# One row product moved from VectorE to GpSimd and ScalarE, the mixes put behind the masks, the last norm on VectorE, one norm's statistics in two parts

## The chip, the cores and the metric

One NeuronCore of one Trainium2 chip runs the whole program. The metric is the device time of one execution in microseconds (us); lower is better. Engines are named PE (TensorE matmul), PEld (TensorE weight load), DVE (VectorE), ACT (ScalarE), POOL (GpSimd) and SP (SyncE, which here only issues DMAs).

## What is computed

One block of a transformer over x of shape 8 x 1024 x 128, all float32. `mod` comes from a small product of `c`. The inner functions, cut to what matters:

```python
h = layernorm(x) * (1 + ca) + sa            # ca, sa: 128 channels, one set per batch
q, k, v, g = h @ Wq.T, h @ Wk.T, h @ Wv.T, h @ Wg.T     # 8 heads, 64 / 64 / 128 / 128 wide
q, k = rotary(q), rotary(k)
o = (q k^T / 8 * decay, causal) v           # retention, no softmax, per head
o = (o - mean) * rsqrt(var + eps) * gn_weight + gn_bias
x = x + ga * ((o * silu(g)) @ Wo.T)
h = layernorm(x) * (1 + cb) + sb
xr, xk = mix of h[t] and h[t-1] by mu_r, mu_k
x = x + gb * (sigmoid(xr @ W_r.T) * (relu(xk @ W_k.T)**2 @ W_v.T))
```

## The kernel before

The 8192 tokens are 64 chunks of 128 (`NCHUNK`), four chunks make a group of 512 tokens (`NGROUP` = 16), two groups a batch. The five engines run five programs that are written out by hand: a prologue, then a loop over `steps` in which every engine does a fixed list of pieces, and a tail for the last group. `due(step - 11, GC, LAST)` says in which step of its engine a piece for a group or chunk comes. Engines meet only through semaphores, so the order of an engine's list is the order in which it works, and a wait stops all that stands behind it on that engine.

In a step PE transposes keys (`transpose_k`), does the causal part of a chunk's retention (`attend`), the scores of the next (`scores`), the part from the running state (`recall`), the new state, the projections q, v, gate, k, and the output projection of older heads. `attend(i)` writes the two PSUM banks `O_E` and `O_O`, and for that it waits until the heads of chunk i-1 were read out of them: `norm_heads(i-1)` on DVE, semaphores `n_E` and `n_O`. The way there starts at the end of `recall(i-1)`: ACT squares (L803), DVE sums (L1145), POOL adds and takes the power -1/2 (`head_rstd`, L1442 and L1445), DVE multiplies (`norm_heads`, L1152).

The first layer norm has two forms. Groups 0 to 3 normalize x by rows and turn it on PE. Groups 4 to 15 (`BY_ROWS`) turn only the statistics: they go through DRAM and come back spread over all partitions (`row_of[:, 0, :]` is the reciprocal deviation, `row_of[:, 1, :]` the shift), while x itself is loaded already turned (`x_turned`, channels on partitions). For these twelve groups

- ACT `scale_rows` (L764) multiplies and shifts `row_of[:, 1, :]` by the channels' factors,
- DVE `apply_rows` (L1071) does `h_full = x_turned * (1 + ca) * row_of[:, 0, :]`,
- POOL `add_rows` (L1410) adds `row_of[:, 1, :]`,
- ACT `round_h` and POOL `low_h` (L1404) split it in a high and a low part for the projections.

In the second half of the block `mix_shift_r` and `mix_shift_k` (DVE, L1164 and L1170) make the two mixes, `round_mix` (ACT, L847) rounds the second, and `split_mix` (DVE, L1179) takes the rest. `mask` (DVE, L1125) puts the causal mask on the scores; `norm_stats` (DVE, L1051 and L1054) takes mean and variance of a group.

The tail does the last group in two parts of two chunks: residual, statistics (DVE), `last_rstd` (POOL), `last_apply` (ACT, L864), `last_transpose` (PE, L548), `last_modulate` (ACT, L884), `last_mix` (DVE, L1229 and L1232), two products, `last_square`, a third product, `last_product` (DVE, L1245 and L1249), store. `keep_busy` are matmuls whose result nobody reads, put before the two `last_transpose`.

## Time and profile before

| | |
|---|---|
| time, median of 3 runs | 751.33 us (750.21 to 752.49) |
| the profiled execution's own time | 750.83 us |
| its span, first to last instruction | 749.0 us |
| PE, PEld busy | 98%, 86% |
| DVE, ACT, POOL busy | 81%, 64%, 81% |
| granted TensorE clock | full in every slice |

The span is what the views of the trace show; the 1.8 us between it and the time lie around it. Busy shares are means over stages that differ, so the views by stretch and by wait are read beside them.

### The profile page before, as it was taken

The numbers are of one execution on the slowest core, as the hardware profiler recorded it, in microseconds if no ns is written. First come the engines' busy times: TensorE is split into PE (matmuls) and PEld (weight loads), VectorE is DVE, ScalarE is ACT, GpSimd is POOL, SyncE is SP. The second block draws the span as 40 slices with busy tenths as digits, with TensorE's granted clock in tenths as the row PEclk, the third lists the DMA queues.
The fourth block names the chain that finished last, engine by engine and source line by source line (L and its number), as shares of the span: only waits on it lengthen the run. The fifth ranks groups of instructions, "written<-read, shape, count | busy, mean of one in ns | idle before, by whom it ended". The sixth has DMA issues, their size and how long they took to land.

```text
span 749.0 us, 29004 instructions
## 1 busy us (share of the span) xinstructions
PE 735.4 (98%) x12123; PEld 643.0 (86%) x12123; DVE 605.7 (81%) x1265; ACT 482.4 (64%) x932; POOL 604.3 (81%) x655
## 2 busy tenths in 40 slices
PE   8989999999999999999999999999999999999997
PEld 7778888888889889888888988988888888988886
DVE  4997688878888887988888898887898878787546
ACT  4566666575665666666666665766666666656665
POOL 5877779789698897988889797888979889787641
PEclk9999999999999999999999999999999999999999
DMA  7611020200202121030211303021020201001001
GB/s 249 193 31 20 13 59 10 65 18 16 79 17 79 25 73 30 10 93 13 75 25 26 81 13 87 9 79 31 13 84 17 73 16 30 18 9 31 24 15 29
DMA packets 59809, 35.15 MB, mean 47 GB/s; under 512 B 36664, under 2 KB 54432, under 8 KB 59680
## 3 DMA queue, kind: packets, MB, share of 16 engines
q1 hardware_dynamic: 58960, 32.51, 16.8%
q8 instruction: 96, 1.57, 0.9%
q10 hardware_dynamic: 720, 0.80, 0.3%
q14 instruction: 33, 0.27, 0.1%
HBM read 20.66 MB, written 4.25 MB: 33 GB/s over the span
## 4 chain that ended last, share of the span: by engine, by line
PE 81%; DVE 10%; issue 3%; ACT 2%; POOL 2%; DMA 1%; SPq 0%; DVEq 0%
PE ring L332 45%; PE outs L332 13%; PE O_E L332 12%; PE ring L347 7%; PE O_O L332 2%; DVE gn_sum L1145 2%; DVE N L1152 1%; DVE delta L1170 1%; ACT N L803 1%; DVE S L1139 1%; DMA N<-in_w_vT 1%; PE ring L397 1%; DVE mix_r L1164 1%; DVE rot_k L1115 1%; DVE sin_k L1118 1%
## 5 line engine op out<-in xcount | busy, mean ns | idle before, releaser
L1452 POOL TENSOR_TENSOR y<-y,gate 128x512 f32<-128x512 f32 x120 | 152.4, 1287 | 29.4 <-ACT y L815 29.4
L1435 POOL TENSOR_TENSOR rot_k<-rot_k,sin_k 128x256 f32<-128x256 f32 x128 | 106.2, 850 | 26.5 <-DVE sin_k L1118 25.8
L332 PEld LDWEIGHTS outs<-wo_gated,y 128*128 128x128 f32 x992 | 119.8, 192 | 6.7 <-DVE y L1191 0.5
L779 ACT ACTIVATE v<-ring 64x512 f32<-64x512 f32 x128 | 76.0, 594 | 75.3 <-PE ring L332 74.3
L332 PE MATMUL outs<-wo_gated,y 128*128 128x128 f32 x992 | 121.7, 275 | 0.1
L1145 DVE TENSOR_REDUCE gn_sum<-N 128x4 f32<-128x512 f32 x118 | 75.5, 681 | 43.4 <-ACT N L803 43.4
L1445 POOL TENSOR_TENSOR gn_rstd<-gn_var,minus_half 128x8 f32<-128x8 f32 x64 | 105.3, 1645 | 5.0
L787 ACT ACTIVATE kT<-ring 128x512 f32<-128x512 f32 x64 | 38.3, 598 | 103.0 <-PE ring L347 103.0
L815 ACT ACTIVATE y<-ring,gn 128x512 f32<-128x512 f32 x126 | 90.9, 777 | 5.2 <-PE ring L347 5.2
L1125 DVE TENSOR_TENSOR A<-ring,consts 128x256 f32<-128x256 f32 x128 | 48.2, 417 | 56.2 <-PE ring L332 56.2
L1429 POOL TENSOR_TENSOR qT<-qT,swapped 128x512 f32<-128x512 f32 x60 | 77.2, 1287 | 14.8 <-DVE swapped L1101 14.6
L808 ACT ACTIVATE gate<-ring 128x512 f32<-128x512 f32 x128 | 76.8, 601 | 3.6 <-PE ring L332 1.2
L1139 DVE TENSOR_TENSOR S<-ring,S 128x512 f32<-128x512 f32 x112 | 76.8, 685 | 2.9 <-PE ring L332 1.0
L332 PE MATMUL O_E<-v,A 64*64 64x128 f32 x992 | 68.0, 275 | 0.6 <-DVE N L1152 0.6
L332 PE MATMUL O_O<-v,A 64*64 64x128 f32 x992 | 68.0, 275 | 0.0
L332 PE MATMUL ring<-v,rot_k 64*64 64x128 f32 x960 | 67.5, 270 | 0.3 <-DVE A L1125 0.3
L332 PE MATMUL ring<-v,k_odd 64*64 64x128 f32 x960 | 67.1, 269 | 0.0
L332 PE MATMUL O_E<-S,qT 64*64 64x128 f32 x928 | 65.3, 269 | 0.1
L332 PE MATMUL O_O<-S,qT 64*64 64x128 f32 x928 | 64.6, 269 | 0.0
L332 PEld LDWEIGHTS ring<-v,rot_k 64*64 64x64 f32 x960 | 57.6, 133 | 0.8 <-issue 0.8
L332 PEld LDWEIGHTS ring<-v,k_odd 64*64 64x64 f32 x960 | 57.9, 133 | 0.0
L332 PEld LDWEIGHTS O_E<-v,A 64*64 64x64 f32 x992 | 53.1, 132 | 4.8 <-DVE N L1152 0.7
(199 smaller groups left out, 2107.9 us busy)
## 6 DMA issues: line engine op xcount, KB each, us to landing
k_odd<-rot_k SPq DMA_DIRECT2D x128, 64.0 KB, 2.2
row_of<-written_rows SPq DMA_DIRECT2D x12, 512.0 KB, 4.0
X<-in_x SPq DMA_DIRECT2D x16, 256.0 KB, 4.3
out<-X SPq DMA_DIRECT2D x15, 256.0 KB, 2.4
x_turned<-in_xT SPq DMA_DIRECT2D x12, 256.0 KB, 4.4
key_tables<-in_const SPq DMA_DIRECT2D x7, 256.0 KB, 5.1
rotary_q<-in_const_q SPq DMA_DIRECT2D x2, 512.0 KB, 6.4
gates<-stored_rows SPq DMA_DIRECT2D x8, 128.0 KB, 3.1
```

Of the source, the lines that this page charges most:

```text
L332: return e.matmul(o, lhsT, rhs, start=start, stop=stop, skip_group_check=True)
L347: done = e.transpose(bank[:, at_column:at_column + HALF], tokens[rows, :], ident[rows, rows])
L779: done = e.activation(v[halves(half), i % 2, 1, :, :], by(PAIRS, bank_of["v", odd, i][halves(1 - half), :]), ACT.Copy)
L808: e.activation(gate[:, n % 2, :], bank_of["gate", n][:, :], ACT.Silu).then_inc(sem["gate"])
L815: e.activation(in_halves(by(GC, y[:, n % NY, :])), from_halves(bank_of["n", n // 2], n % 2, GC), ACT.Identity, bias=gn[:, 1, h:h + 1], sca ...
L1125: e.tensor_tensor(A[:, odd, :, :], by(PAIRS, bank_of["kT", i][:, odd, W // 2:W]), causal.unsqueeze(1).broadcast_to([P, PAIRS, HALF]), ALU. ...
L1139: e.tensor_tensor(new, added, old, ALU.add).then_inc(sem["S"])
L1145: e.tensor_reduce(gn_sum[:, i % 2, odd, :], N[:, i % NN, odd, :, :], AXIS.X, ALU.add).then_inc(sem["sum_" + eo])
L1429: e.tensor_tensor(q, q, swapped[:, :], ALU.add).then_inc(sem["qT"])
L1435: done = e.tensor_tensor(turned[:, n, :, :], turned[:, n, :, :], sin[:, n, :, :], op)
L1445: e.tensor_tensor(gn_rstd[:, i % 2, :, :].rearrange("p e a -> p (e a)"), gn_var[:, i % 2, :, :].rearrange("p e a -> p (e a)"), minus_half[ ...
L1452: e.tensor_tensor(y[:, n % NY, :], y[:, n % NY, :], gate[:, n % 2, :], ALU.mult).then_inc(sem["y"])
```

## The change

Five things are edited.

1. `apply_rows` moves from DVE to POOL and loses the factor by channels; that factor becomes an activation on ACT in `scale_rows`, in place on `x_turned`. `add_rows` stays on POOL, but stands between the two `gate_head` of its step and no longer in front of `rotate_k`.
2. In the loop DVE does `mix_shift_k` behind the two masks, and ACT does `round_mix` behind the squares of the next step.
3. In the tail `last_apply` is a two-scalar operation on DVE (subtract the mean, multiply by the reciprocal deviation); the negated mean and the shift go away; the mix r, the relu and the tanh are written in another order; the last `ffn_out` goes from POOL to DVE; 2 + 3 idle matmuls stand where 5 + 4 stood.
4. `norm_stats` is split in `norm_stats` and `norm_mv`. In the prologue the statistics of group 2 are taken right behind `add_state(0)`, and only `norm_mv(2, 0)` stays where both were.
5. In the prologue the masks of chunk 2 stand in front of `norm_heads(0, 1)`.

The diff, cut (the semaphores that come and go are left out):

```diff
         def scaled_rows(g):
-            return 2 * (g - BY_ROWS) + 2
+            return 3 * (g - BY_ROWS) + 3
...
-            keep_busy(O[1][:, :, :].rearrange("p n v -> p (n v)"), 5, True)
+            keep_busy(O[1][:, :, :].rearrange("p n v -> p (n v)"), 2, True)
             last_transpose(0)
-            keep_busy(O[1][:, :, :].rearrange("p n v -> p (n v)"), 4, True)
+            keep_busy(O[1][:, :, :].rearrange("p n v -> p (n v)"), 3, True)
             last_transpose(1)
             last_k(0)
+            last_k(1)
             last_r(0)
-            last_k(1)
...  scalar, scale_rows
                 at.wait_ge("rows_read", 32 * (g - BY_ROWS + 1))
+                e.activation(x_turned[:, :], x_turned[:, :], ACT.Copy, scale=mod_cols[:, 1, b:b + 1]).then_inc(sem["rows_act"])
                 e.activation(row_of[:, 1, :], row_of[:, 1, :], ACT.Identity, bias=mod_cols[:, 0, b:b + 1],
...  scalar, loop
                 for i in due(step, 1, NCHUNK, 4):
                     square(i, 1)
+                for g in due(step - 10, GC, LAST):
+                    round_mix(g)
...
-                for g in due(step - 9, GC, LAST):
-                    round_mix(g)
...  vector
-            def apply_rows(g):
-                e.scalar_tensor_tensor(out=h_full[:, :], in0=x_turned[:, :], scalar=mod_cols[:, 1, b:b + 1], in1=row_of[:, 0, :],
-                                       op0=ALU.mult, op1=ALU.mult).then_inc(sem["rows_applied"])
...
+            def last_apply(part):
+                at.wait_ge("last_rstd", part + 1)
+                at.wait_ge("n0T", NGROUP)
+                at.wait_ge("n1T", LAST)
+                for j in range(GC)[chunks_of(part)]:
+                    e.tensor_scalar(normed[:, j, :], X[:, LAST % NX, j, :], ln_mv[:, 1, j, 0:1], ln_rstd[:, 1, j:j + 1],
+                                    ALU.subtract, ALU.mult).then_inc(sem["last_apply"])
...
+            def last_ffn_out():
+                xg = X[:, (LAST - 1) % NX, :, :]
+                e.tensor_tensor(xg, xg, product, ALU.add).then_inc(sem["ffn_out"])
...  vector, prologue
             add_state(0)
+            norm_stats(2, 0)
             rotate_k(2)
...
             norm_heads(0, 0)
-            norm_heads(0, 1)
             mask(2, 1)
             mask(2, 0)
+            norm_heads(0, 1)
             rotate_q(5)
             add_state(2)
-            norm_stats(2, 0)
+            norm_mv(2, 0)
...  vector, loop
-                for g in due(step - 11, GC, LAST):
-                    mix_shift_k(g)
...
                 for i in due(step, 1, NCHUNK, 5):
                     mask(i, 0)
+                for g in due(step - 11, GC, LAST):
+                    mix_shift_k(g)
...
-                for g in due(step + 6, GC, NGROUP, BY_ROWS):
-                    apply_rows(g)
...  gpsimd
+            def apply_rows(g):
+                at.wait_ge("rows_read", 32 * (g - BY_ROWS + 1))
+                at.wait_ge("rows_act", scaled_rows(g))
+                e.tensor_tensor(h_full[:, :], x_turned[:, :], row_of[:, 0, :], ALU.mult).then_inc(sem["rows_applied"])
...
                 for g in due(step + 8, GC, NGROUP, BY_ROWS):
-                    add_rows(g)
+                    apply_rows(g)
                 for i in due(step + 4, 1, NCHUNK, 7):
                     rotate_k(i)
...
                     gate_head(2 * i)
+                for g in due(step + 8, GC, NGROUP, BY_ROWS):
+                    add_rows(g)
...
             last_rstd(1)
-            ffn_out(LAST - 1)
```

POOL's list in the step of a group by rows (`y` is `gate_head`, `rot_k` is `rotate_k`, `gn_rstd` is the power in `head_rstd`), before:

```order
L1461 TENSOR_TENSOR delta<-h2T 128x512
L1429 TENSOR_TENSOR qT<-qT,swapped 128x512
L1410 TENSOR_TENSOR h_full<-h_full,row_of 128x512
L1435 TENSOR_TENSOR rot_k<-rot_k,sin_k 128x16x16 x2
L1452 TENSOR_TENSOR y<-y,gate 128x512 x2
L1442 TENSOR_TENSOR gn_var<-gn_sum,consts 128x8
L1445 TENSOR_TENSOR gn_rstd<-gn_var,minus_half 128x8
```

and the same place of the changed kernel:

```order
L1477 TENSOR_TENSOR delta<-h2T 128x512
L1445 TENSOR_TENSOR qT<-qT,swapped 128x512
L1422 TENSOR_TENSOR h_full<-x_turned,row_of 128x512
L1451 TENSOR_TENSOR rot_k<-rot_k,sin_k 128x16x16 x2
L1468 TENSOR_TENSOR y<-y,gate 128x512
L1426 TENSOR_TENSOR h_full<-h_full,row_of 128x512
L1468 TENSOR_TENSOR y<-y,gate 128x512
L1458 TENSOR_TENSOR gn_var<-gn_sum,consts 128x8
L1461 TENSOR_TENSOR gn_rstd<-gn_var,minus_half 128x8
```

One instruction of 128x512 more stands between `qT` and `gn_rstd`. On ACT, the step before that one has the scaling of the rows and a second-half norm (`normed`) in front of the copy of the turned keys (`kT`); in the changed kernel:

```order
L783 ACTIVATE v<-ring 128x512
L809 ACTIVATE gate<-ring 128x512
L764 ACTIVATE x_turned<-x_turned,mod_cols 128x512
L765 ACTIVATE row_of<-row_of,mod_cols 128x512
L751 ACTIVATE normed<-X,ln_rows 128x128 x4
L788 ACTIVATE kT<-ring 128x2x4x64
```

The `x_turned` row is new, the others stood there in the same order. The end of DVE's list, changed kernel, from the statistics of the second part (`swapped` is the mix k and later its square, `turned` the mix r and later the tanh):

```order
L1200 BN_STATS ln_stats<-X 128x6 x2
L1203 BN_AGGR ln_mv<-ln_stats 128x2 x2
L1211 TENSOR_SCALAR normed<-X,ln_mv,ln_rows 128x128 x2
L1172 SCALAR_TENSOR_TENSOR delta<-mix_r,ring 128x512
L1211 TENSOR_SCALAR normed<-X,ln_mv,ln_rows 128x128 x2
L1222 TENSOR_TENSOR h_full<-h2T 128x256
L1224 SCALAR_TENSOR_TENSOR swapped<-h_full,mu,h2T 128x256
L1222 TENSOR_TENSOR h_full<-h2T 128x256
L1224 SCALAR_TENSOR_TENSOR swapped<-h_full,mu,h2T 128x256
L1229 SCALAR_TENSOR_TENSOR turned<-h_full,mu,h2T 128x256
L1241 TENSOR_TENSOR swapped<-swapped 128x256
```

The four `normed` are new on DVE. Behind these rows come the second mix r, the second square, the 128x512 addition of the last `ffn_out`, and two pairs of `last_product`.

## Rows read from the trace of the kernel before

**Rows 1.** The page, part 1: busy us, share and instructions of each engine.

```profile
PE 735.4 (98%) x12123; PEld 643.0 (86%) x12123; DVE 605.7 (81%) x1265; ACT 482.4 (64%) x932; POOL 604.3 (81%) x655
```

**Rows 2.** Stretches: length, busy us and instructions of PE, PEld, DVE, ACT, POOL.

```profile
300.00:400.00 100.00, 99.91 (x1696) 87.87 (x1694) 85.82 (x173) 65.48 (x118) 87.55 (x96) 1.00 0.17 41
...
700.00:749.00 49.00, 43.88 (x504) 37.52 (x502) 28.38 (x66) 30.64 (x58) 19.37 (x23) 1.00 0.07 20
```

**Rows 3.** Timeline of POOL, 427 to 448: start, us, instruction, [idle before <-releaser].

```profile
427.32 1.42 POOL L1435 TENSOR_TENSOR rot_k<-rot_k,sin_k 128x256 f32<-128x256 f32 x2 [0.52 <-DVE sin_k L1118]
...
430.05 1.28 POOL L1452 TENSOR_TENSOR y<-y,gate 128x512 f32<-128x512 f32 x1 [1.31 <-ACT y L815]
...
439.59 1.33 POOL L1410 TENSOR_TENSOR h_full<-h_full,row_of 128x512 f32<-128x512 f32 x1
440.88 2.33 POOL L1435 TENSOR_TENSOR rot_k<-rot_k,sin_k 128x256 f32<-128x256 f32 x2
443.18 2.54 POOL L1452 TENSOR_TENSOR y<-y,gate 128x512 f32<-128x512 f32 x2
...
445.97 1.65 POOL L1445 TENSOR_TENSOR gn_rstd<-gn_var,minus_half 128x8 f32<-128x8 f32 x1
```

**Rows 4.** Timeline of DVE in the same step.

```profile
439.71 1.76 DVE L1164 SCALAR_TENSOR_TENSOR mix_r<-delta,mu,h2T 128x512 f32<-128x512 f32 x1
...
448.25 0.68 DVE L1152 TENSOR_TENSOR N<-O_O,gn_rstd 128x512 f32<-128x512 f32 x1
```

**Rows 5.** Timelines: PE's next attend, then POOL and PE one group later.

```profile
449.91 0.32 PE L332 MATMUL O_E<-v,A 64*64 64x128 f32 x1
...
490.40 1.65 POOL L1445 TENSOR_TENSOR gn_rstd<-gn_var,minus_half 128x8 f32<-128x8 f32 x1
...
494.59 0.32 PE L332 MATMUL O_E<-v,A 64*64 64x128 f32 x1
```

**Rows 6.** Timelines, last chunk: POOL's power and the attend that waits for it.

```profile
708.58 1.64 POOL L1445 TENSOR_TENSOR gn_rstd<-gn_var,minus_half 128x8 f32<-128x8 f32 x1
...
711.68 0.29 PE L332 MATMUL O_E<-v,A 64*64 64x128 f32 x1 [0.60 <-DVE N L1152]
```

**Rows 7.** Timelines of ACT and PEld, the step before a step by rows.

```profile
426.54 1.64 ACT L751 ACTIVATE normed<-X,ln_rows 128x128 f32<-128x128 f32 x4
428.64 0.60 ACT L787 ACTIVATE kT<-ring 128x512 f32<-128x512 f32 x1 [0.46 <-PE ring L347]
...
429.34 0.38 PEld L332 LDWEIGHTS ring<-qT,kT 64*64 64x64 f32 x16
```

**Rows 8.** Groups by form, 200 to 700: busy us, mean ns, idle before.

```profile
L764 ACT ACTIVATE row_of<-row_of,mod_cols 128x512 f32<-128x512 f32 x10 | 8.2, 823 | 0.0
...
L770 ACT ACTIVATE hT_hi<-h_full 128x512 fp32r<-128x512 f32 x10 | 6.2, 622 | 0.0
...
L1164 DVE SCALAR_TENSOR_TENSOR mix_r<-delta,mu,h2T 128x512 f32<-128x512 f32 x11 | 15.3, 1394 | 0.0
...
L1071 DVE SCALAR_TENSOR_TENSOR h_full<-x_turned,mod_cols,row_of 128x512 f32<-128x512 f32 x10 | 7.4, 739 | 0.0
```

**Rows 9.** Timelines of DVE and PE in the prologue.

```profile
27.30 0.69 DVE L1115 TENSOR_TENSOR rot_k<-ring,key_tables 128x512 f32<-128x512 f32 x1 [0.74 <-PE ring L332]
...
41.60 0.86 DVE L1051 BATCH_NORM_STATS2 ln_stats<-X 128x6 f32<-128x128 f32 x4
42.38 0.36 DVE L1054 BATCH_NORM_AGGREGATE ln_mv<-ln_stats 128x2 f32<-128x6 f32 x4
...
43.97 0.47 PE L347 MATMUL ring<-consts,rot_k 64*128 64x64 f32 x8 [1.16 <-DVE qT L1098]
```

**Rows 10.** Timelines of ACT and DVE in the tail.

```profile
738.42 0.88 ACT L864 ACTIVATE normed<-X,ln_rows 128x128 f32<-128x128 f32 x2
...
740.54 0.62 DVE L1229 TENSOR_TENSOR h_full<-h2T 128x256 f32<-128x256 f32 x1 [1.28 <-ACT h2T L884]
...
746.26 0.42 DVE L1249 TENSOR_TENSOR X<-X,h_full 128x256 f32<-128x256 f32 x1
```

More of the change, by code:

```diff
@@ L857, in load_tables @@
                 e.dma_start(key_tables[:, c, :, :, :].rearrange("p k h d -> p (k h d)"), columns).then_inc(sem[tables(c)[0]], 16)
-            def last_apply(part):
-                at.wait_ge("last_shift", part + 1)
-                at.wait_ge("n0T", BY_ROWS)
-                at.wait_ge("n1T", LAST)
-                for j in range(GC)[chunks_of(part)]:
-                    e.activation(normed[:, j, :], X[:, LAST % NX, j, :], ACT.Identity, bias=ln_shift[:, 1, j:j + 1],
-                                 scale=ln_rstd[:, 1, j:j + 1]).then_inc(sem["last_apply"])
             def last_scale(part):
@@ L997, in _ @@
                 last_relu(part)
+            for part in range(PARTS):
                 last_act_r(part)
@@ L1217, in last_stats @@
                 done.then_inc(sem["last_mv"])
-                at.wait_ge("last_mv", part + 1)
-                e.tensor_scalar(ln_neg[:, 1, these], ln_mv[:, 1, these, 0], -1.0, None, ALU.mult).then_inc(sem["last_neg"])
+            def last_apply(part):
[5 more added lines that the diff above has]
+                                    ALU.subtract, ALU.mult).then_inc(sem["last_apply"])
             def last_mix(part):
@@ L1230, in last_mix, with last_mix_r @@
                 at.wait_ge("last_delta", part + 1)
-                for n, what in ((1, "k"), (0, "r")):
-                    e.scalar_tensor_tensor(out=last_mixed[what][:, cols], in0=last_delta[:, cols], scalar=mu[:, n:n + 1], in1=before,
-                                           op0=ALU.mult, op1=ALU.add).then_inc(sem["last_mix_" + what])
+                e.scalar_tensor_tensor(out=last_mixed["k"][:, cols], in0=last_delta[:, cols], scalar=mu[:, 1:2], in1=before,
+                                       op0=ALU.mult, op1=ALU.add).then_inc(sem["last_mix_k"])
+            def last_mix_r(part):
+                cols = tokens_of(part)
+                e.scalar_tensor_tensor(out=last_mixed["r"][:, cols], in0=last_delta[:, cols], scalar=mu[:, 0:1],
+                                       in1=h2T[:, 1, cols], op0=ALU.mult, op1=ALU.add).then_inc(sem["last_mix_r"])
+            def last_ffn_out():
+                xg = X[:, (LAST - 1) % NX, :, :]
+                at.wait_ge("product", LAST)
+                at.wait_ge("ffn_out", LAST - 1)
+                e.tensor_tensor(xg, xg, product, ALU.add).then_inc(sem["ffn_out"])
             def last_square(part):
@@ L1354, in _ @@
             last_stats(1)
+            last_apply(0)
             ffn_product(LAST - 1)
+            last_apply(1)
             last_mix(0)
             last_mix(1)
+            last_mix_r(0)
             last_square(0)
+            last_mix_r(1)
             last_square(1)
+            last_ffn_out()
             last_product(0)
@@ L1476, in last_rstd @@
                                 ).then_inc(sem["last_rstd"])
-                at.wait_ge("last_rstd", part + 1)
-                at.wait_ge("last_neg", part + 1)
-                e.tensor_tensor(ln_shift[:, 1, these], ln_neg[:, 1, these], ln_rstd[:, 1, these], ALU.mult
-                                ).then_inc(sem["last_shift"])
             e.memset(minus_half[:, :], -0.5)
```

21 lines of the change are left out of this document (11 added, 10 removed).

## The prediction

> **What bounds the kernel now.** I read the page's busy shares first. PE has 98%, DVE and POOL 81% each, ACT 64% [rows 1]. The table of stretches then says where PE is not full: from 300 to 400 us it is busy 99.91 of 100 us, in the last 49 us 43.88 [rows 2]. So in the loop nothing done faster on another engine can shorten the time; only a delay that reaches PE can change it, upward. Gains can lie in the prologue and in the tail.
>
> The question for the loop is how much room each step leaves PE. I went through the timelines of POOL, DVE and PE step by step. PE starts `attend` of a chunk when DVE has normed the heads of the chunk before, and DVE needs POOL's `gn_rstd` for that. In the step in which POOL adds the rows, POOL has no idle time from 430.05, where it waited for ACT's y, to the end of `gn_rstd` at 445.97 + 1.65 = 447.62 [rows 3]. PE begins the next attend at 449.91 [rows 5], 2.29 us after it. One group later `gn_rstd` ends at 492.05 and PE begins at 494.59, 2.54 us later [rows 5]. Eleven steps have this form (attends from 182 to 628 us): six with 2.29 to 2.32, five with 2.53 to 2.55. The first of the twelve groups by rows, at 138 us, has 3.7.
>
> How little is enough is seen at the last chunk, where PE really waits: `gn_rstd` ends at 708.58 + 1.64 = 710.22, PE starts at 711.68 [rows 6], so 1.46 us are used by two multiplications of DVE and the signals. The room is therefore 2.29 - 1.46 = 0.83 us in six steps and 2.54 - 1.46 = 1.08 in five.
>
> **The rows on POOL.** In front of `gn_rstd` one more product of 128x512 comes on POOL. The same kind with the same operands' size takes 2.50 us for two, start to end of the y pair (443.18 to 445.68), so 1.25 each [rows 3]. Nothing hides it, since POOL has no idle time there. The sum 1.25 - 0.83 gives 0.42 us of new wait of PE in six steps, 1.25 - 1.08 gives 0.17 in five: 2.5 + 0.85 = **3.4 us**. Behind the waiting `attend` stands all of PE's list, and PE is the bound, so it isn't given back. The add between the two `gate_head` changes the place of a delay, not its length; its second y ends near 447, and PE reads it with the output projection behind the first one at about 448, so that is still in time.
>
> What DVE saves there is its own product, 739 ns [rows 8]. It stood before the norm of the odd heads in the step before, on an engine that isn't waited for there. I cost that at nothing; its cover is POOL's queue, which is what comes last.
>
> Does it relieve POOL? DVE and POOL slow each other: the mixes (`mix_r` 1394 ns on average) take nearly twice the 739 ns of the same instruction in `apply_rows` [rows 8], and the `rot_k` beside them takes 2.33 us where one beside no mix takes 1.42 [rows 3], as DVE's `mix_r` from 439.71 lasts 1.76 [rows 4]. So it is the mixes that POOL pays for, 0.91 us, and the removed product paid nothing extra. The Trainium skill, "SBUF — State Buffer", section "Who interferes with whom", has the rule: a VectorE instruction with two SBUF inputs and a GpSimd instruction that reads SBUF lock each other out for a whole instruction. By that rule the removal of a two-input instruction from VectorE speaks for the change; the row of 739 ns says that here it met no long POOL instruction. The two mixes remain, and POOL is busy wherever they fall, so moving mix k behind the masks moves its 0.4 to 0.5 us and doesn't remove it. That is the first rival below.
>
> **The factor by channels on ACT.** It comes in the step before, in front of `row_of`, four `normed` and the copy of the turned keys. Its duration isn't in the trace: a copy of that size without pointer operands takes 622 ns, one with two (scale and bias) 823 [rows 8]; this one has one, I take the middle, 720, and by the pipelining seen between `normed` (until 428.18) and its neighbours it takes about 0.1 less of ACT's time, 0.62; the bounds are 0.52 and 0.72. The Trainium skill, "ScalarE: Activation LUTs", section "What ACT_TABLE_LOAD costs", says that each [128,1] pointer operand adds about 93 ns; 622 + 93 would be 715, and the rows agree. ACT had 0.46 us idle in front of `kT` [rows 7]. So the copy comes 0.16 late (0.06 to 0.26). It ended at 429.24, and PE loaded the first of these weights at 429.34 [rows 7]; with a signal of 0.05, 0.05 are free. PE waits 0.11 (0.01 to 0.21), twelve times: **1.3 us** (0.1 to 2.5). POOL's chain starts behind ACT's y in this same step [rows 3], so it is late by the part that PE doesn't share, 0.05 in eleven steps: **0.5 us**.
>
> **Mix k and its rounding.** In the loop the masks wait for PE anyway, and the rounding's wait for DVE goes away in front of ACT's squares. Both shorten the way to the sums, but in the steps by rows POOL takes the sums late, and that way is not what PE waits for. Zero in the loop; without the cover it would be a gain of some tenths in five steps, counted in the rival.
>
> **Prologue.** PE idles 1.16 us before 43.97, for a bank that DVE's rotation releases [rows 9]. DVE is busy without pause from 27.3 to there. The statistics of group 2, 41.60 to 42.38, go to 26.6, where DVE idled 0.74 us for PE [rows 9]; x of that group has landed by then. DVE reaches the rotation 0.78 earlier, POOL's reciprocal deviation too. What follows up to 60 us hangs on DVE in the same order. Gain **0.8 us**, the 0.78 of the row (0.2 if the idle time at 26.6 takes less of it; 1.2, the whole of PE's wait, with what the earlier masks of chunk 2 add).
>
> **Tail.** ACT's two `normed` run from 738.42 to 739.30, DVE's first delta starts at 740.54, and the last addition ends at 746.68 [rows 10]. DVE can begin `normed` at 738.3, without the shift on POOL (0.2) and without ACT. I take 0.25 each from the statistics' size, so the first part is ready at 738.8; PE is past its last real products and two idle matmuls at 739.0, transposes until 739.4, ACT gives h2T at 739.95, DVE's delta starts at 740.0. The second part follows at 741.0 where it was 742.3. From there DVE is the bound. Two deltas and two mixes k at 0.46 each, with a wait for the second part (until 741.95), two mixes r and two squares of 0.40 to 0.45 (until 743.7), the `ffn_out` that came from POOL, 0.68 like the 128x512 of [rows 4], then the four of `last_product`, 1.75. That ends at 746.1. Gain **0.55 us** (1.3 if the `ffn_out` falls in a wait; a loss of 0.2 if its 256 KB store, now at 744.4, delays the last ones).
>
> **Sum.** 3.4 + 1.3 + 0.5 - 0.8 - 0.55 = +3.85 on the profiled execution's 750.83 (span 749.0 and 1.8 around it), so 754.7; that execution is 0.5 below the median of 751.33. On the median it is **755.2 us**, 0.5% slower. With the low bounds (PE's wait at the keys 0.1, prologue 1.2, tail 1.3, no lag of POOL's chain) it is +1.0, 752.3; with the high ones (2.5, 0.2, and +0.2) +6.4, 757.7.
>
> **Rivals.** What a measurement can tell from no change is about 0.3%, 2.25 us, so 749.1 to 753.6.
>
> *POOL is relieved.* If the mixes no longer meet POOL's chain, POOL gets back the 0.91 us, the new product costs 0.34, less than the room of 0.83, and PE waits in no step by rows. Left are the keys (0.1 to 1.3), the prologue and the tail: 0 to -1.25. With the tail at its best (0.75 more) and some 0.25 us of small waits gone from PE in the five steps of the second kind, where DVE's sums come earlier, it is -3.3: 748.0. It decides from 0.42 us less in POOL's chain on. For it speaks that the mixes are spread out; against it that POOL has no pause in the stretch, so that a mix must displace something.
>
> *A part only.* The 1.25 us are partly hidden, or ACT's copy costs nothing, and the three gains stand: +1 to +2, 753.
>
> *The delay spreads.* POOL leaves the step 1.25 us late, and the next step's chain, with 4.5 us from `gn_rstd` to attend, has room. But the second y, the low part of h for the next group and the released banks come late as well; if one of them stops PE by another 0.3 us in each of the eleven steps, +7: 758.5.
>
> *The change doesn't do what it says* can't be here; the lists show each move.
>
> **How the numbers follow.** The forecast (waits of PE in the steps by rows, +1.0 to +6.4) 0.55, nearly all of it slower by over 0.3%; a part only 0.17, within; POOL relieved 0.20, of it 0.12 faster by over 0.3% and 0.08 within; the delay spreads 0.08, slower. With 0.01 of the forecast within, faster is 0.12, same 0.26, slower 0.62. The range is 748.8 to 758.0, which leaves out the best part of the relief and most of the spread; the forecast alone has 752.3 to 757.7.
>
> **What the profile after would show.** In a step by rows POOL without a pause, `gn_rstd` ending 1.3 us later against PE's earlier attend, and a wait of PE "O_E <- DVE N" of 0.2 to 0.5, eleven times; the waits before the scores for ACT's `kT` near 0.1, twelve times; the gap before the transposes of chunk 3 near 0.4 to 0.7 instead of 1.16; DVE the chain from 740 on. The prediction is wrong if `gn_rstd` is followed by the attend in more than 1.46 us in these steps, or if `rot_k` beside the mixes falls to 1.42.

## The result, and the profile after

The changed kernel takes 753.38 us (median of 22 executions, 752.17 to 756.4); the kernel before, on the same chips, 751.14 (22 executions, 750.04 to 753.5). The ratio is 1.0034, 95% interval [1.0025, 1.0043]: about 2.5 us slower. The profiled executions differ by 2.2 us of span, 751.2 after against 749.0.

The page's shares of the kernel after, to be held against [rows 1]:

```profile
PE 733.0 (98%) x12119; PEld 644.2 (86%) x12119; DVE 598.8 (80%) x1256; ACT 488.1 (65%) x940; POOL 616.8 (82%) x664
```

DVE has 6.9 us less, POOL 12.5 more, ACT 5.7 more. No engine is full, so this says little; the chain that ended last says more. It follows the work back from the last instruction, with each engine's share of the span, and by line. First the shares before, then both lines after:

```profile
PE 81%; DVE 10%; issue 3%; ACT 2%; POOL 2%; DMA 1%; SPq 0%; DVEq 0%
```

```profile
PE 74%; DVE 10%; POOL 9%; issue 4%; ACT 1%; DMA 1%; ACTq 0%; DVEq 0%
PE ring L332 41%; PE O_E L332 12%; PE outs L332 12%; PE ring L347 6%; POOL y L1468 4%; PE O_O L332 3%; POOL gn_rstd L1461 3%; DVE N L1139 2%; POOL h_full L1426 2%; DVE gn_sum L1132 1%; DVE delta L1157 1%; DVE A L1112 1%; PE ring L397 1%; DMA consts<-in_const 1%; DVE wffn_v L1033 1%
```

POOL's part has grown from 2% to 9%: its products y, `gn_rstd`, and the addition of the rows. PE's waits say where it enters. After, the list of what PE waited for begins with

```profile
PE O_E L332 <- DVE N L1139: 5.6, 11, 0.8
PE ring L347 <- DVE sin_k L1105: 1.1, 1, 1.1
```

Before, the attend waited once in this way, for 0.6 us [rows 6]. Now it is eleven times, 5.6 us together: in ten of the eleven steps by rows, and again at the last chunk. The same stretch as in [rows 2]:

```profile
300.00:400.00 100.00, 99.11 (x1693) 87.79 (x1692) 84.21 (x170) 66.45 (x119) 89.28 (x97) 1.00 0.15 41
```

PE is 0.80 us less busy than before in these 100 us, POOL 1.73 more. Here is POOL's timeline in the step that [rows 3] show, with the two multiplications of DVE and the attend that hang on it:

```profile
440.26 1.33 POOL L1445 TENSOR_TENSOR qT<-qT,swapped 128x512 f32<-128x512 f32 x1
441.54 1.74 POOL L1422 TENSOR_TENSOR h_full<-x_turned,row_of 128x512 f32<-128x512 f32 x1
443.23 1.98 POOL L1451 TENSOR_TENSOR rot_k<-rot_k,sin_k 128x256 f32<-128x256 f32 x2
445.17 1.31 POOL L1468 TENSOR_TENSOR y<-y,gate 128x512 f32<-128x512 f32 x1
446.44 1.29 POOL L1426 TENSOR_TENSOR h_full<-h_full,row_of 128x512 f32<-128x512 f32 x1
447.68 1.30 POOL L1468 TENSOR_TENSOR y<-y,gate 128x512 f32<-128x512 f32 x1
448.94 0.21 POOL L1458 TENSOR_TENSOR gn_var<-gn_sum,consts 128x8 f32<-128x8 f32 x1
449.23 1.65 POOL L1461 TENSOR_TENSOR gn_rstd<-gn_var,minus_half 128x8 f32<-128x8 f32 x1
...
450.91 0.69 DVE L1139 TENSOR_TENSOR N<-O_E,gn_rstd 128x512 f32<-128x512 f32 x1 [3.15 <-POOL gn_rstd L1461]
451.51 0.68 DVE L1139 TENSOR_TENSOR N<-O_O,gn_rstd 128x512 f32<-128x512 f32 x1
...
452.34 0.29 PE L332 MATMUL O_E<-v,A 64*64 64x128 f32 x1 [0.84 <-DVE N L1139]
```

POOL works without a pause. DVE sits idle for 3.15 us until `gn_rstd` ends at 450.88, and PE starts 1.46 us after that, the bare minimum of the last chunk [rows 6], where it had 2.29 before. In ten of the eleven steps this distance is now 1.46 or 1.47.

In the steps of one kind the wait is longer than what the step grows by. The next such step grows by 0.18, and its attend waits 0.50:

```profile
497.19 0.29 PE L332 MATMUL O_E<-v,A 64*64 64x128 f32 x1 [0.50 <-DVE N L1139]
```

With the rows' part alone (`e2_rows_only`, below) that wait is 0.10 or 0.12. The other 0.4 is time that item 2 saved earlier in the same step (shown under the mixes), and PE now spends it waiting here.

Where the 2.2 us of span come from is read off the starts of the 64 attends, each against its counterpart before. The steps by rows from 182 to 628 us are longer by 0.41, 0.18, 0.41, 0.18, 0.43, 0.18, 0.83, 0.18, 0.40, 0.16 and -0.01, together +3.35. (Of the 0.83, which is the step shown, about 0.4 is there once: ahead of these rows POOL idles 0.26 us for nothing that the trace names, and its `qT` and `rot_k` take 0.06 and 0.11 longer than in the other steps of this kind. Why stays open.) The first attend came 0.22 late, and by attend 9 the shift was -0.47, a gain of 0.69; attends 10 and 11 gave +0.11; single steps and the last attend +0.17. The last attend is 3.16 late, and the span ends only 2.2 late, so 0.96 came back in the tail. The 0.22 goes with the clock: in the first 15 us the mean granted clock is 0.89, before it was 1.00. It is no part of the change: in the profiled executions of all fourteen kernels the first attend comes 0 to 0.33 early where those 15 us have 1.00 (five kernels), 0.02 to 0.57 late where they have 0.89 (eight, among them `e2_rows_only` and `e4_factor_on_act`, whose start is the one of before), and 1.38 late at 0.77 (`e5_mixes_only`).

### The profile page after: what moved, and what is told of

Read it like the earlier page. It is cut to its first block, busy times and chain, and to the rows that moved or that the text cites. A ratio compares the mean times of both kernels' runs of the same rounds, so it can differ in the third digit from the quotient of the medians.

```text
span 751.2 us, 29021 instructions
## 1 busy us (share of the span) xinstructions
PE 733.0 (98%) x12119; PEld 644.2 (86%) x12119; DVE 598.8 (80%) x1256; ACT 488.1 (65%) x940; POOL 616.8 (82%) x664
## 3 DMA queue, kind: packets, MB, share of 16 engines
q8 instruction: 96, 1.57, 0.9%
## 4 chain that ended last, share of the span: by engine, by line
PE 74%; DVE 10%; POOL 9%; issue 4%; ACT 1%; DMA 1%; ACTq 0%; DVEq 0%
PE ring L332 41%; PE O_E L332 12%; PE outs L332 12%; PE ring L347 6%; POOL y L1468 4%; PE O_O L332 3%; POOL gn_rstd L1461 3%; DVE N L1139 2%; POOL h_full L1426 2%; DVE gn_sum L1132 1%; DVE delta L1157 1%; DVE A L1112 1%; PE ring L397 1%; DMA consts<-in_const 1%; DVE wffn_v L1033 1%
## 5 line engine op out<-in xcount | busy, mean ns | idle before, releaser
L1468 POOL TENSOR_TENSOR y<-y,gate 128x512 f32<-128x512 f32 x120 | 156.8, 1320 | 30.0 <-ACT y L816 29.9
L1451 POOL TENSOR_TENSOR rot_k<-rot_k,sin_k 128x256 f32<-128x256 f32 x128 | 102.1, 819 | 27.2 <-DVE sin_k L1105 25.8
L1139 DVE TENSOR_TENSOR N<-O_E,gn_rstd 128x512 f32<-128x512 f32 x62 | 42.2, 681 | 31.8 <-POOL gn_rstd L1461 31.7
```

The lines of the kernel that those rows point to most:

```text
L1139: e.tensor_tensor(N[:, i % NN, odd, :, :], heads_of(i)[odd], rstd, ALU.mult).then_inc(sem["n_" + eo])
L1451: done = e.tensor_tensor(turned[:, n, :, :], turned[:, n, :, :], sin[:, n, :, :], op)
L1468: e.tensor_tensor(y[:, n % NY, :], y[:, n % NY, :], gate[:, n % 2, :], ALU.mult).then_inc(sem["y"])
```

## The experiments

Twelve kernels. Each was timed beside the kernel before on the same chip; a shift of an attend is taken from the profiled execution against that of before. "Steps by rows" are the same eleven as above, six of a first kind (10.62 to 10.65 us long before, the last one 10.48) and five of a second (10.81 or 10.82).

### The rows' part alone, and everything but it

`e1_rows_back` is the changed kernel with item 1 undone:

```diff
 ACT scale_rows
-                e.activation(x_turned[:, :], x_turned[:, :], ACT.Copy, scale=mod_cols[:, 1, b:b + 1]).then_inc(sem["rows_act"])
 DVE loop, between norm_heads(i, 0) and norm_heads(i, 1)
+                for g in due(step + 6, GC, NGROUP, BY_ROWS):
+                    apply_rows(g)
 POOL loop
-                    apply_rows(g)
+                    add_rows(g)
 ...
                     gate_head(2 * i)
-                for g in due(step + 8, GC, NGROUP, BY_ROWS):
-                    add_rows(g)
```

> The changed kernel with the rows' product back on VectorE and ScalarE's factor by channels gone; mixes behind the masks, prologue and tail stay changed. Theory (the product in POOL's chain is the whole loss, 3.35 us in the steps by rows; prologue and tail give back 0.65 and 0.96): about -1.5 us against the kernel before, 749.7, and the eleven steps by rows as long as before. Rival (the mixes or the order of the edits cost part of it): between -1 and +1.5 us, and some steps by rows stay longer than before.

Measured: 747.92 us against 750.94, ratio 0.9961 [0.9948, 0.9973], -3.0 us: twice the gain that my theory gave. The steps by rows are not as long as before but shorter, by 2.13 us in all: 0.38 to 0.40 in four of the second kind and 0.26 in the last, the others 0.01 to 0.09. So the rest of the change has a gain in the loop that the changed kernel did not show. The tail's part is as expected (last attend at -1.53, span 2.53 shorter, so 1.0).

`e2_rows_only` is the kernel before with item 1 alone, the reverse of that diff on the other kernel.

> The kernel before with the rows' part alone: factor on ScalarE, product on POOL, addition between the two gate_heads. Theory: +3.35 us, 754.5, PE waiting for the normed heads in the eleven steps by rows by 0.41 and 0.17. Rival (mix k behind the masks is what brings VectorE against POOL's product, or spares it): a loss that is smaller or larger than 3.35 by over 0.7 us.

Measured: 753.95 against 750.94, ratio 1.0041 [1.0029, 1.0054], +3.0 us. The steps by rows take 2.93 us more, 0.37 to 0.40 in four of the first kind, 0.68 in the one near 450 us (again an extra of 0.3), nothing in the last, and 0.13 to 0.15 in the second kind. So item 1 on the kernel before costs 2.9. Put on a kernel that has the other items, it costs 3.35 + 2.13 = 5.5, since it also takes their gain.

`e4_factor_on_act` is the kernel before with only the factor on ACT; DVE keeps a plain product.

```diff
 ACT scale_rows
+                e.activation(x_turned[:, :], x_turned[:, :], ACT.Copy, scale=mod_cols[:, 1, b:b + 1]).then_inc(sem["rows_act"])
 DVE apply_rows
+                at.wait_ge("rows_act", scaled_rows(g))
-                e.scalar_tensor_tensor(out=h_full[:, :], in0=x_turned[:, :], scalar=mod_cols[:, 1, b:b + 1], in1=row_of[:, 0, :],
-                                       op0=ALU.mult, op1=ALU.mult).then_inc(sem["rows_applied"])
+                e.tensor_tensor(h_full[:, :], x_turned[:, :], row_of[:, 0, :], ALU.mult).then_inc(sem["rows_applied"])
```

> The kernel before with the factor by channels on ScalarE alone; the product stays on VectorE as a plain multiplication. Theory from the changed kernel's trace: kT comes at most 0.06 us later, PE loses nothing, 0.0 to +0.3 us. Rival (the term of the prediction): twelve waits of 0.11 us and a late chain on POOL, +1.3 to +1.8 us.

Measured: 750.36 against 750.94, ratio 0.9994 [0.9986, 1.0003]. The term of the prediction, +1.3 us, is outside this interval, and so is +1.8 with the late chain. Nor does the trace show the late chain: `gn_rstd` ends 2.30 to 2.33 us before the attend in the first kind of step and 2.55 or 2.56 in the second, no later than before. ACT in the changed kernel, in the step of [rows 7]:

```profile
427.43 0.74 ACT L764 ACTIVATE x_turned<-x_turned,mod_cols 128x512 f32<-128x512 f32 x1
428.04 0.83 ACT L765 ACTIVATE row_of<-row_of,mod_cols 128x512 f32<-128x512 f32 x1
428.75 1.65 ACT L751 ACTIVATE normed<-X,ln_rows 128x128 f32<-128x128 f32 x4
430.30 0.58 ACT L788 ACTIVATE kT<-ring 128x512 f32<-128x512 f32 x1
```

The copy takes 0.61 of ACT's time (427.43 to 428.04), as forecast. But `kT` now has no idle time ahead of it, and it starts at 430.30, 0.10 before the `normed` ahead of it ends (430.40). Before, it stood alone behind 0.46 of idle. A back-to-back start is worth another 0.10, so the room was 0.56, and `kT` is 0.05 late, what PE had free. PE's side agrees, in `e4_factor_on_act` and in the changed kernel alike: in each of these steps `kT` starts 0.15 to 0.18 behind the attend and not 0.11, yet the scores that need it start 0.92 behind the attend, as in every step before. None of the twelve waits is there.

### Is it the product, or its place?

`e3_idle_spot` is the changed kernel with POOL's product one step earlier, where POOL waits 1.35 us for ACT's y.

```diff
 POOL loop
-                for g in due(step + 8, GC, NGROUP, BY_ROWS):
-                    apply_rows(g)
                 for i in due(step + 4, 1, NCHUNK, 7):
                     rotate_k(i)
+                for g in due(step + 9, GC, NGROUP, BY_ROWS):
+                    apply_rows(g)
```

> The changed kernel with POOL's product one step earlier, between rotate_k and the first gate_head, where POOL idles 1.35 us for ScalarE's y (430.35 to 431.70). Theory (what costs is the place in a chain without a pause, not the product's engine): the waits of the steps by rows go, about 749.8, -1.5 us against before, as with the product on VectorE. Rival (more work on POOL costs wherever it stands, because it makes the other engine's instructions wait for SBUF or because POOL's slack is used up a step later): +0.5 us or more against before.

Measured: 748.55 against 750.94, ratio 0.997 [0.9959, 0.9981], -2.4 us. The waits for N are gone from the steps by rows, with POOL doing all of the added work. So it is the place. But only 0.06 us is left of the 2.13 that `e1_rows_back` gained there. About 1.3 of the difference is made up at attends 10 and 11 (below).

`e8_product_twice` does the product twice in its place in the chain, `e9_half_in_chain` leaves half of its columns there and does the other half at the idle spot.

```diff
 e8, POOL apply_rows
                 e.tensor_tensor(h_full[:, :], x_turned[:, :], row_of[:, 0, :], ALU.mult).then_inc(sem["rows_applied"])
+                at.wait_ge("rows_applied", 2 * (g - BY_ROWS) + 1)
+                e.tensor_tensor(h_full[:, :], x_turned[:, :], row_of[:, 0, :], ALU.mult).then_inc(sem["rows_applied"])
 e9, POOL loop
                 for g in due(step + 8, GC, NGROUP, BY_ROWS):
-                    apply_rows(g)
+                    apply_rows(g, 1)
 ...
                     rotate_k(i)
+                for g in due(step + 9, GC, NGROUP, BY_ROWS):
+                    apply_rows(g, 0)
```

> The changed kernel with POOL's product of each group by rows done twice, one behind the other, in the same place. Theory (in eleven steps POOL's queue up to gn_rstd is what PE waits for, without any room left): each of them 1.25 to 1.75 us longer and one or two more at the ends, +14 to +20 us against the changed kernel, 768 to 773. Rival (something else, such as ScalarE's factor or the mixes, sets these steps): less than +8 us.

> The changed kernel with POOL's product cut in two halves of columns: one in POOL's idle time one step earlier, between rotate_k and gate_head, the other left in front of the chain. With the product away, gn_rstd ended 2.15 and 2.24 us before the next attend, and 1.46 of these are needed: 0.69 and 0.78 of room. Theory (a threshold: only what goes beyond that room is waited for, and half a product is about 0.63 to 0.65 us): no wait of PE for the normed heads, steps by rows about 2 us shorter than before in all, and the first group's gap gone too, 747. Rival (each piece of work in that chain costs in proportion): half of 3.35 + 2.13 = 5.5 us comes back, 750.

Measured: `e8_product_twice` 770.06 against 750.76, ratio 1.0251 [1.0237, 1.0265], 16.7 us more than the changed kernel. (Some 2 us of it is not the product's: three of its four executions had a mean granted clock of 0.995 and took 770.0 to 770.1, the profiled one had 0.999 and took 767.66. By the traces the last attend is 14.6 later than in the changed kernel.) The steps by rows grow by 1.56 to 1.62 in four of the first kind and 1.48 to 1.50 in the second over before, where the single product gave 0.41 and 0.18: 1.2 and 1.3 for one product more, and no step has room. `e9_half_in_chain` 747.65 against 750.87, ratio 0.9959 [0.9947, 0.9971]: half a product costs nothing in the steps by rows. Before the attend `gn_rstd` ends 1.53 to 1.57 us in the first kind (2.13 in the last of them) and 1.47 to 1.50 in the second, just short of being waited for, and the steps are 2.27 us shorter than before in all. So it is a threshold, not a price per us of work.

### The mixes behind the masks

`e5_mixes_only` is the kernel before with item 2 alone.

```diff
 DVE loop
-                for g in due(step - 11, GC, LAST):
-                    mix_shift_k(g)
 ...
                 for i in due(step, 1, NCHUNK, 5):
                     mask(i, 0)
+                for g in due(step - 11, GC, LAST):
+                    mix_shift_k(g)
 ACT loop
                     square(i, 1)
+                for g in due(step - 10, GC, LAST):
+                    round_mix(g)
 ...
                     scale_head(2 * i + 1)
-                for g in due(step - 9, GC, LAST):
-                    round_mix(g)
```

> The kernel before with one part alone: mix k behind the masks and its rounding in front of ScalarE's list. With the rows' product back on VectorE the changed kernel had its steps by rows 2.13 us shorter in all than the kernel before, nearly all of it in the five of the second kind (0.26 to 0.40 each), where PE waits about 0.3 us for the second bank of S before its second projection. Theory (that is this part's gain, since VectorE reaches the additions of S earlier): -2.1 us, 749.0. Rival (the part is worth nothing, as the prediction had it for the loop, and the 2.13 us came of another edit): 0.0 +- 0.3 us.

Measured: 749.05 against 750.76, ratio 0.9976 [0.9967, 0.9985], -1.7 us. The steps by rows are 1.81 shorter in all: 0.38 to 0.40 in four of the second kind, while the fifth is 0.15 longer; attend 11 is 0.42 later. (This profiled execution began at the low clock named above and took 750.38, 1.3 over the median, so its span is no measure.) Why the fifth step is longer stays open. This part has the gain. What it removes is not in the list of waits, since it hides in the modelled length of a matmul. Before, PE's matmuls around the second projection v in a step of the second kind, and DVE:

```profile
488.99 0.40 PE L332 MATMUL ring<-hT_hi,wg_lo 128*128 128x512 f32 x1
489.49 0.50 PE L332 MATMUL ring<-wv_hi,hT_hi 128*128 128x512 f32 x1
489.82 0.40 PE L332 MATMUL ring<-wv_lo,hT_hi 128*128 128x512 f32 x1
...
484.72 1.65 DVE L1170 SCALAR_TENSOR_TENSOR delta<-delta,mu,h2T 128x512 f32<-128x512 f32 x1
486.29 0.74 DVE L1125 TENSOR_TENSOR A<-ring,consts 128x256 f32<-128x256 f32 x2
487.55 1.28 DVE L1145 TENSOR_REDUCE gn_sum<-N 128x4 f32<-128x512 f32 x2 [0.52 <-ACT N L803]
488.75 1.41 DVE L1139 TENSOR_TENSOR S<-ring,S 128x512 f32<-128x512 f32 x2
```

The pitch of these matmuls is 0.23, but from 488.99 to 489.49 it is 0.50: PE waits for the bank that the first of DVE's two additions of S releases (it ends near 489.45). The matmul behind the pause takes another 0.10 more than its pitch, 0.33. With the rows' product back and the mixes behind the masks (`e1_rows_back`):

```profile
488.15 0.40 PE L332 MATMUL ring<-hT_hi,wg_lo 128*128 128x512 f32 x1
488.39 0.40 PE L332 MATMUL ring<-wv_hi,hT_hi 128*128 128x512 f32 x1
...
485.24 0.98 DVE L1164 SCALAR_TENSOR_TENSOR delta<-delta,mu,h2T 128x512 f32<-128x512 f32 x1
486.15 1.26 DVE L1139 TENSOR_REDUCE gn_sum<-N 128x4 f32<-128x512 f32 x2
487.34 1.40 DVE L1133 TENSOR_TENSOR S<-ring,S 128x512 f32<-128x512 f32 x2
```

Counted from the step's attend (483.77 before, 482.94 here), S begins at 4.98 and at 4.40. The mix (named `delta`, its output) was 1.65 long in front of the masks and stood between PE's scores and DVE's answer; behind them it takes 0.98 and fills the time in which DVE waited for ACT.

Why then did `e3_idle_spot` not have it? Its PE, DVE and POOL in the same step, from its attend on:

```profile
481.88 0.32 PE L332 MATMUL O_E<-v,A 64*64 64x128 f32 x1
...
487.66 0.50 PE L332 MATMUL ring<-wv_hi,hT_hi 128*128 128x512 f32 x1 [0.17 <-DVE S L1126]
...
484.18 1.63 DVE L1157 SCALAR_TENSOR_TENSOR delta<-delta,mu,h2T 128x512 f32<-128x512 f32 x1
...
483.99 1.28 POOL L1468 TENSOR_TENSOR y<-y,gate 128x512 f32<-128x512 f32 x1
485.22 1.75 POOL L1426 TENSOR_TENSOR h_full<-h_full,row_of 128x512 f32<-128x512 f32 x1
...
486.93 1.40 DVE L1126 TENSOR_TENSOR S<-ring,S 128x512 f32<-128x512 f32 x2
```

The mix lasts until half a microsecond after the end of POOL's y (485.27), and POOL's addition, which began in that time, takes 1.75 and not 1.28. S begins 5.05 behind the attend, no earlier than the 4.98 of before, and here PE's wait for it is named. `e10_add_in_front` tests it: the only edit against `e3_idle_spot` is the addition, back in front of `rotate_k` as before the change.

```diff
 POOL loop
+                for g in due(step + 8, GC, NGROUP, BY_ROWS):
+                    add_rows(g)
                 for i in due(step + 4, 1, NCHUNK, 7):
                     rotate_k(i)
 ...
                     gate_head(2 * i)
-                for g in due(step + 8, GC, NGROUP, BY_ROWS):
-                    add_rows(g)
```

> The changed kernel with POOL's product at its idle spot one step earlier, and POOL's addition in front of rotate_k, where it was before the change, and not between the two gate_heads. With the addition between them, mix k behind the masks met it and took 1.63 us in the second kind of step, and PE waited there for S as before. Theory (the meeting of this mix with that long POOL instruction costs the gain of the moved mixes): mix k near 1.0 us, the five steps of the second kind 0.4 shorter each, 746.7, 1.9 us less than with the addition between the gate_heads. Rival (POOL's total work, 1.25 us more per group, is what keeps VectorE late): 748.5, no change.

Measured: 746.65 against 750.87, ratio 0.9946 [0.9934, 0.9959], -4.2 us; it is the fastest of all. The mix:

```profile
483.42 0.95 DVE L1157 SCALAR_TENSOR_TENSOR delta<-delta,mu,h2T 128x512 f32<-128x512 f32 x1
...
483.10 1.87 POOL L1451 TENSOR_TENSOR rot_k<-rot_k,sin_k 128x256 f32<-128x256 f32 x2
```

It now meets a POOL product of half the size and is over after 0.95. The steps by rows are 2.23 shorter than before in all, with the same work on POOL as in `e3_idle_spot`. The Trainium skill, "SBUF — State Buffer", section "Who interferes with whom", calls the shared port pair an exclusive lock and says that issue order decides who blocks. The rows agree: one and the same instruction takes 0.74 where POOL runs nothing beside it, 0.95 beside half a `rot_k`, and 1.63 beside a whole y that began 0.19 before it.

### The first group by rows

`e7_first_behind` is `e1_rows_back` with the product of the first of the twelve groups behind DVE's `rotate_k`.

```diff
 DVE loop
-                for g in due(step + 6, GC, NGROUP, BY_ROWS):
+                for g in due(step + 6, GC, NGROUP, BY_ROWS + 1):
                     apply_rows(g)
 ...
                     rotate_k(i)
+                for g in due(step + 6, GC, BY_ROWS + 1, BY_ROWS):
+                    apply_rows(g)
```

> The changed kernel with the rows' product back on VectorE, and of the twelve only the first one moved behind rotate_k. In the kernel before that product met POOL's qT product at 123.6 us, each of the two took 1.57 and 1.72 us, and PE then idled 0.99 us at 127.08 for the rotated keys. Theory (the wait comes from this product standing in front of rotate_k in that one step): 1.2 us less than with all twelve in front, 746.7, and no idle time of PE near 127. Rival (the wait comes from POOL's qT and rotation being late anyway, or is given back one step later, as the 1.30 us of the changed kernel at attend 11): 747.9.

Measured: 746.86 against 750.76, ratio 0.9949 [0.9937, 0.9962], -3.9 us. Before, DVE, POOL and PE in that one step (DVE's `rot_k` and `sin_k` follow and end at 126.97):

```profile
123.61 1.57 DVE L1071 SCALAR_TENSOR_TENSOR h_full<-x_turned,mod_cols,row_of 128x512 f32<-128x512 f32 x1
...
124.59 1.72 POOL L1429 TENSOR_TENSOR qT<-qT,swapped 128x512 f32<-128x512 f32 x1
...
127.08 0.47 PE L347 MATMUL ring<-consts,rot_k 64*128 64x64 f32 x8 [0.99 <-issue]
```

The idle time of 0.99 is gone in this kernel, and from attend 9 to attend 10 this kernel takes 1.20 less than `e1_rows_back`. Attend 11 gives 0.28 of it back (+0.70 against +0.42; PE idles 0.49 there for DVE's `sin_k`), so 0.9 is left. In the changed kernel, where the product is not on DVE, the gap is gone too (1.20 from attend 9 to 10), but attend 11 loses 1.30: PE waits 1.09 for `sin_k`, the second of the waits quoted above. POOL's queue is behind this one as well. DVE's `rot_k` and `sin_k` stand behind its N, and N waits 1.20 for `gn_rstd`. With the product at the idle spot (`e3_idle_spot`) attend 11 loses 0.29, with two products in the chain 2.65. So the first group pays about 1.0 for the product in its place, through a wait for the keys and not for the normed heads.

### Prologue and tail

`e11_prologue_only` is the kernel before with items 4 and 5 alone, `e6_tail_only` with item 3 alone. The core of each edit:

```diff
 e11, DVE
+            norm_stats(2, 0)
             rotate_k(2)
 ...
-            norm_heads(0, 1)
             mask(2, 1)
             mask(2, 0)
+            norm_heads(0, 1)
 ...
-            norm_stats(2, 0)
+            norm_mv(2, 0)
 e6, DVE
+            last_apply(0)
             ffn_product(LAST - 1)
+            last_apply(1)
             last_mix(0)
             last_mix(1)
+            last_mix_r(0)
             last_square(0)
+            last_mix_r(1)
             last_square(1)
+            last_ffn_out()
```

> The kernel before with the prologue's part alone: statistics of group 2 taken apart and moved ahead, the norm of the odd heads behind the masks of chunk 2. Theory from the traces (attend 2 came 0.26 and attend 3 0.19 earlier in the kernels with this part): -0.45 us, 750.4. Rival (the prediction's term): -0.8 us; the other: a gain that is lost again by attend 14, 0.0.

> The kernel before with the tail's part alone: last normed on VectorE, the mixes k of both halves ahead of the mixes r, the last ffn_out on VectorE, PE's order. The loop stays as before. Theory from the changed kernel's trace (the span grew 0.96 us less than the last attend's shift): -0.9 to -1.1 us, 750.1. Rival (the prediction's term): -0.55 us, and up to +0.2 if the store of the last group but one delays the last ones.

Measured: `e11_prologue_only` 750.36 against 750.87, ratio 0.9993 [0.9984, 1.0001], which tells 0.45 neither from nothing nor from 0.8. Its trace has the steps: attend 2 comes 0.25 earlier, attend 3 0.10 later. But the last attend is where it was, since attends 45 and 53 come 0.31 and 0.14 later (in most kernels attend 45 comes 0.22 earlier), and the span is 749.0 as before. So this kernel shows the gain at attend 2 and not in its time. In five of the kernels with this part attend 3 came 0.18 to 0.21 earlier as well, in four 0.10 or 0.11 later, so the part is worth 0.15 to 0.45 us. (Attend 9 stands at -0.44, but 0.18 at attend 6 and 0.10 at attend 7 are there in kernels without this part too and belong to the one execution of before.) `e6_tail_only` 749.95 against 750.76, ratio 0.9989 [0.998, 0.9998], -0.8 us; the last attend is 0.20 late and the span 0.8 shorter, so the tail has 1.0, as in every other kernel that has this part whole (0.97 to 1.01).

`e12_ffn_out_on_pool` is `e10_add_in_front` with the one addition of the tail back on POOL.

```diff
 DVE
-            last_ffn_out()
 POOL
             last_rstd(1)
+            ffn_out(LAST - 1)
```

> The kernel with the product at POOL's idle spot and the addition in front, and in the tail the ffn_out of the last group but one back on POOL, everything else of the tail as changed. Theory (VectorE is the tail's bound, and POOL is idle there): 0.5 to 0.6 us less than with it on VectorE, 746.1. Rival (POOL's addition meets VectorE's deltas and mixes, and each waits for the other): no gain or a loss up to 0.6, 746.7 to 747.3.

Measured: 748.16 against 750.87, ratio 0.9964 [0.9951, 0.9978], 1.5 us slower than `e10_add_in_front`; by the traces the span is 0.74 longer, 0.63 of it behind the last attend. My theory fell, and the rival stands. First `e12_ffn_out_on_pool`, then `e10_add_in_front`:

```profile
736.15 1.55 DVE L1211 TENSOR_SCALAR normed<-X,ln_mv,ln_rows 128x128 f32<-128x128 f32 x2
737.62 0.41 DVE L1222 TENSOR_TENSOR h_full<-h2T 128x256 f32<-128x256 f32 x1
...
736.31 1.31 POOL L1475 TENSOR_TENSOR X<-X,delta 128x512 f32<-128x512 f32 x1 [0.28 <-DVE delta L1172]
```

```profile
736.04 0.60 DVE L1211 TENSOR_SCALAR normed<-X,ln_mv,ln_rows 128x128 f32<-128x128 f32 x2
```

DVE's second pair of `normed` takes 1.55 us beside POOL's addition and 0.60 without it, and the whole tail hangs on this pair. The remaining 0.8 us between the medians goes with the clock of the whole execution. The six times of `e12_ffn_out_on_pool` are 746.71 to 747.37 in the three executions whose mean granted clock is 0.998 or 1.0, and 748.95 to 749.9 in the three that have 0.993 to 0.995; `e10_add_in_front` has 746.42 to 747.26, all at 0.997 or more.

## Why the prediction was right, and which of its terms were off

The forecast was 755.2 with a range of 748.8 to 758.0, 3.85 us above before; measured were 753.38 and 2.2 above. The mechanism of the largest term was right, the other two costs were not there. So what came true is, nearly to the number, the rival *A part only* ("ACT's copy costs nothing, and the three gains stand: +1 to +2, 753"), which had a chance of 0.17.

- **The rows on POOL, 3.4 us**: measured 3.35 in the changed kernel, with 0.41 and 0.18 where 0.42 and 0.17 were worked out. Part of that match is luck: a one-off of 0.4 near 450 us makes up for the last step, which gave -0.01 and not a wait. The list of waits is longer (4.9 us in ten steps), because it also holds the gain of item 2. The rule behind it, room 0.83 and 1.08 over the minimum of 1.46, holds: half a product costs nothing, one more costs 1.2 to 1.3 per step. What the prediction left out is the first of the twelve groups, which it set aside for its distance of 3.7 us: it pays 1.0 as well, by way of DVE's rotation of the keys.
- **The factor on ACT, 1.3 us, and the late chain behind it, 0.5**: the step that failed. Alone it measured 0.9994 [0.9986, 1.0003], and the scores start 0.92 behind the attend with it as without it. Its duration was right (0.61 against 0.62 of ACT's time). The room was not: 0.46 of idle time ahead of `kT` are 0.56 of room, since back to back it starts 0.10 before its predecessor's end. The lateness left, 0.05, is what PE had free, as the prediction itself had found. The late chain isn't there either: in nine of the eleven steps of the changed kernel `gn_rstd` starts 7.94 (first kind) or 7.88 (second) us behind the attend ahead of it, where it was 6.69 and 6.63, later by 1.25, which is the product alone.
- **DVE relieved of its product at no gain**: right in the steps by rows, wrong for the first group, where that product did meet POOL and took 1.57. "The removed product paid nothing extra" came from an average of ten, out of 200 to 700 us, that left this one out. The changed kernel had no use of it, since attend 11 took it back (1.20 gained, 1.30 lost).
- **Mix k, zero in the loop**: right for this kernel, by the reason given (POOL's chain comes last). Without that cover the prediction put "some tenths in five steps"; measured were 0.38 to 0.40 in four and 0.26 in the fifth (`e1_rows_back`), alone -1.7 us.
- **Relief of POOL**: against it spoke that POOL has no pause and a mix must displace something. So it was. In the first kind of step `rot_k` takes 1.87 and not 2.33, but the y behind it 1.75 and not 1.28. Before, and then after, in the step near 355 us:

```profile
351.73 2.33 POOL L1435 TENSOR_TENSOR rot_k<-rot_k,sin_k 128x256 f32<-128x256 f32 x2
```

```profile
352.70 1.87 POOL L1451 TENSOR_TENSOR rot_k<-rot_k,sin_k 128x256 f32<-128x256 f32 x2
354.53 1.75 POOL L1468 TENSOR_TENSOR y<-y,gate 128x512 f32<-128x512 f32 x1
```

  In the second kind nothing moved: the product takes 1.72 where the addition took 1.73, and `rot_k` takes 1.88 in both. So the net cost of 1.25 us per step came out as worked out. What the prediction had not seen is that mix k itself becomes shorter when it meets a shorter instruction.
- **Prologue, -0.8**: -0.44 in the changed kernel (attends 2 and 3), 0.15 to 0.45 by the traces of the other kernels, and in the time of `e11_prologue_only` not told from nothing. The wait of 1.16 [rows 9] did fall, to 0.56, but a new one of 0.64 came at 40.28, for DVE's rotation of queries. Which of the two moves brought it wasn't tried.
- **Tail, -0.55**: measured -0.96. DVE in the changed kernel:

```profile
743.03 0.42 DVE L1222 TENSOR_TENSOR h_full<-h2T 128x256 f32<-128x256 f32 x1
743.49 0.48 DVE L1224 SCALAR_TENSOR_TENSOR swapped<-h_full,mu,h2T 128x256 f32<-128x256 f32 x1
744.06 0.43 DVE L1222 TENSOR_TENSOR h_full<-h2T 128x256 f32<-128x256 f32 x1
...
746.62 0.68 DVE L1236 TENSOR_TENSOR X<-X,delta 128x512 f32<-128x512 f32 x1
...
748.46 0.42 DVE L1252 TENSOR_TENSOR X<-X,h_full 128x256 f32<-128x256 f32 x1
```

  On the clock of before (3.16 earlier) the first delta starts at 739.87, forecast 740.0; the second at 740.90, forecast 741.0. From there it works nearly without a pause, as forecast, and ends at 745.72 and not 746.1, because every piece was taken a little too long: the two deltas and mixes k give way to the next at 741.76 (forecast 741.95), the squares at 743.46 (743.7), and what follows takes 2.26 and not 2.43.

Summed with what the runs showed, on the profiled execution of before: 3.35 - 0.45 - 0.96 + 0.25 (start, first group and single steps together) = +2.2.

## What to carry to other kernels

An engine's work is priced at its place in the queue: what stands in a chain without a pause costs all that exceeds the room behind it, and here the same instruction in an idle spot one step earlier cost nothing. Edits do not add up when one decides whether another's wait comes last, so a change of several parts is to be run part by part: this one held a version 0.54% faster than before (`e10_add_in_front`), hidden by two misplaced instructions. Where DVE and POOL both work in SBUF, count not how often they meet but how long the instruction is that is met.

## What the runs showed of the hardware

- One DVE instruction, 128x512 with two inputs in SBUF, took 0.74 or 0.75 us where POOL ran nothing beside it, 0.87 to 1.22 beside POOL's 128x256 products alone, and up to 1.77 beside its 128x512 ones (all fourteen traces; the mixes).
- The pair of 128x128 tensor_scalar with two pointer operands, which reads one large tile only, took 1.55 us in the one kernel where a POOL addition of 128x512 ran beside it, and 0.59 to 0.61 without it.
- ACT's 128x512 copy with one pointer operand took 734 ns on average, between 622 with none and 823 with two [rows 8].
- A wait of PE of 0.27 us stood in no list of waits of the kernel before: it was visible only as a pitch of 0.50 between two matmuls that otherwise start 0.23 apart.
